# State space: the products u in a ring of three places, the third of them in SBUF, and three rows of C instead of four

## The reference, cut to what matters

```
a = jnp.exp(dt[..., None] * A[None, None])
u = dt[..., None] * Bv[:, :, None, :] * xs[..., None]
_, h = jax.lax.associative_scan(_affine_combine, (a, u), axis=1)   # h[t] = a[t] * h[t-1] + u[t]
y = jnp.einsum('btis,bts->bti', h, C) + xs * D_skip[None, None, :]
y = y * _silu(z)
return jnp.einsum('bti,di->btd', y, out_proj_w)
```

## Time and profile before

| | |
|---|---|
| median of 3 runs | 3406.47 us (3404.86 to 3411.97) |
| the profiled execution, its own time | 3401.26 us |
| its span, first to last instruction | 3399.5 us |
| state space: first scan to last scan | 2297.8 to 3381.3 us |
| a middle block of it | about 136 us |
| the last block | about 133 us |
| PE, DVE, ACT, POOL busy over the span | 94%, 82%, 68%, 47% |

### The profile page before, as it was taken

One profiled execution on the slowest core, in us unless ns is written; L12 is line 12 of the kernel. 1 busy time (PEld: TensorE's weight loads), 2 busy tenths in 40 slices (PEclk: granted clock), 3 DMA queues, 4 the chain that ended last, 5 costly groups with the idle time before them and its releaser, 6 DMA issues. The chain is left out here.

```text
span 3399.5 us, 61118 instructions
## 1 busy us (share of the span) xinstructions
PE 3188.7 (94%) x19814; PEld 1279.1 (38%) x19815; DVE 2788.6 (82%) x4945; ACT 2316.7 (68%) x3660; POOL 1601.0 (47%) x2080
## 2 busy tenths in 40 slices
PE   7997999989999999999999999769999999999987
PEld 4654666632222222222222222343334334333333
DVE  6766334689999999999999999258899989898997
ACT  4444333358887887888788788657877767777763
POOL 2113300024444434444333444207888888888885
PEclk9999999989999999999999999889999999999998
DMA  5442211111111110111111010141222222222221
GB/s 169 131 151 91 78 56 53 48 42 29 53 45 40 39 34 27 31 36 36 36 33 34 25 34 27 46 136 59 69 75 81 71 73 69 73 87 66 76 78 50
DMA packets 160889, 211.63 MB, mean 62 GB/s; under 512 B 32324, under 2 KB 108364, under 8 KB 160604
## 3 DMA queue, kind: packets, MB, share of 16 engines
q1 hardware_dynamic: 141340, 172.51, 16.6%
q0 software_dynamic: 8512, 18.76, 1.8%
q10 hardware_dynamic: 10752, 16.78, 1.5%
HBM read 154.48 MB, written 52.69 MB: 61 GB/s over the span
## 5 line engine op out<-in xcount | busy, mean ns | idle before, releaser
L1439 ACT ACTIVATE prob<-psS 128x1024 f32<-128x1024 f32 (+3 forms) x1280 | 1104.0, 906 | 280.2 <-PE psS L1623 270.8
L1489 DVE TENSOR_REDUCE pmax<-psR 128x1 f32<-128x512 f32 x1674 | 1057.2, 684 | 79.9 <-PE psR L1565 47.6
L2265 POOL TENSOR_TENSOR hc<-h_d,crep 128x512 f32<-128x512 f32 x512 | 647.7, 1273 | 186.8 <-DVE h_d L2494 136.5
L1565 PE MATMUL psR<-kslab,qslab 48*128 48x512 bf16 (+3 forms) x2480 | 653.0, 352 | 22.2 <-DVE pmax L1489 14.0
L1638 PE MATMUL psVo<-prob,vaug 128*32 128x512 f32 (+3 forms) x5120 | 630.8, 546 | 1.5 <-ACT ov L1443 0.8
L1623 PE MATMUL psS<-qslab,kslab 51*128 51x512 bf16 (+3 forms) x2560 | 533.4, 353 | 39.8 <-ACT prob L1439 22.6
L2494 DVE TENSOR_TENSOR_SCAN h_d<-a,state,psU 128x512 f32<-128x512 f32 x384 | 489.4, 1275 | 0.0
L1354 POOL TENSOR_SCALAR_AFFINE_SELECT prob<-prob 128x256 f32<-128x256 f32 (+1 forms) x512 | 214.0, 421 | 533.1 <-ACT prob L1439 533.1
L2484 DVE TENSOR_TENSOR psU<-dtx,psX 128x512 f32<-128x512 f32 x512 | 356.0, 695 | 89.6 <-PE psX L2644 38.8
L1565 PEld LDWEIGHTS psR<-kslab,qslab 48*128 48x128 bf16 x2480 | 187.3, 94 | 628.9 <-DVE pmax L1489 473.6
L2397 ACT ACTIVATE a<-dt,a_neg 128x512 f32<-128x512 f32 x512 | 366.7, 723 | 54.5 <-DVE h_d L2494 53.6
(11 more groups left out here) (351 smaller groups left out, 5045.5 us busy)
## 6 DMA issues: line engine op xcount, KB each, us to landing
crep<-c_rows_d SPq DMA_DIRECT2D x256, 256.0 KB, 3.1
x_e<-rows_d SPq DMA_DIRECT2D x72, 128.0 KB, 2.0
y_d<-y SPq DMA_DIRECT2D x72, 128.0 KB, 1.7
q_d<-parts SPq DMA_DIRECT2D x48, 128.0 KB, 2.4
k_d<-parts SPq DMA_DIRECT2D x48, 128.0 KB, 2.3
qslab<-q_d SPq DMA_DIRECT2D x60, 96.0 KB
kslab<-k_d SPq DMA_DIRECT2D x60, 96.0 KB
wg<-n_L_ffn_gate_proj_w_dram ACTq DMA_DIRECT2D x8, 512.0 KB, 4.1
```

Source lines behind the costliest of these rows:

```text
L1439: act.activation(prob[g % BUFS][:, :, off:BLK], psS[g % 2][:, :, off:BLK], ACT.Exp).then_inc(prob_ready, 1)
L1489: dve.tensor_reduce(into[:, lo:lo + (count - 1) * NEXT + 1:NEXT], psR[at % BANKS][:, 0:count * w].rearrange("p (n w) -> p n w", w=w), AX.X ...
L1565: ins = pe.matmul(dst[:, m * w:(m + 1) * w], qslab[u][rows, i * P:(i + 1) * P], kslab[u][rows, ch * BLK:ch * BLK + w], start=(m == 0), sto ...
L2265: pool.tensor_tensor(hc[:, g % CR], h[:, g % HR], crep[:, g // PAIR % SPR], ALU.mult).then_inc(hc_ready, 1)
```

## The change

The product u gets a third place: `u = [psU[0], psU[1], u_sb]`, where `u_sb` is a tile of 128 x 512 float32 in SBUF. Unit g uses place g % 3. `input_term(g)` now waits for `scan(g - 3)` instead of `scan(g - 2)`. Of the 512 units, 170 have their u in SBUF. The SBUF for it comes from the ring of C rows, which shrinks from four places to three; row k of C now waits until POOL has used up row k - 3.

```
-        AR, HR, CR, LAG, SPR = 5, 5, 6, 3, 4
+        AR, HR, CR, LAG, SPR = 5, 5, 6, 3, 3
...
         h = sb("h_d", [P, HR, BLK])
+        u_sb = sb("u_sb", [P, BLK])
...
         psU = [ps(f"psU{i}", [P, BLK]) for i in range(2)]
+        u = [psU[0], psU[1], u_sb]
...
                 dve.wait_ge(dtx_ready, CT * blk + c + 1 + CREDIT)
-                if g >= 2:
-                    dve.wait_ge(h_ready, g - 1 + CREDIT)
-                dve.tensor_tensor(psU[g % 2][:], dtx[:, c], psX[g // PAIR % 2][:], ALU.mult).then_inc(u_ready, 1)
+                if g >= len(u):
+                    dve.wait_ge(h_ready, g - len(u) + 1 + CREDIT)
+                dve.tensor_tensor(u[g % len(u)][:], dtx[:, c], psX[g // PAIR % 2][:], ALU.mult).then_inc(u_ready, 1)
...
-                dve.tensor_tensor_scan(h[:, g % HR], a[:, g % AR], psU[g % 2][:],
+                dve.tensor_tensor_scan(h[:, g % HR], a[:, g % AR], u[g % len(u)][:],
```

## The result

The changed kernel takes 3419.1 us (median of 18 runs, 3412.1 to 3427.5), the one before 3405.5 us (18 runs). The ratio is 1.0045, with a 95% interval of 1.0035 to 1.0056: 14 us slower, a quarter of the 52 us that were forecast. The profiled execution lies at the long end of its runs, 3426.2 us with a span of 3424.4, so what its rows add up to (25 us more than before) is more than the median shows.

The account below looks back on a forecast made before the run. DVE was taken to be close to the limit in every block. Per block, 12.8 us gained against 18.5 us of holds, plus waits, gave 143 instead of 136.3 us: 52 us more in all, forecast 3457 us, range 3325 to 3510.

Parts of the forecast that it names:

- The sum: State space phase: a block takes 143 us, 6.7 more than 136.3, adding 52 us over eight blocks.
- The first term: DVE's time in a block: 118.8 us after the removed wait plus 18.5 us of held scans, 137.3 us.
- the second: DVE's waits for others in a block: 2 to 5 us of the present 6 us stay.
- What bounds the kernel: State space phase: DVE close to the limit in all blocks, busy for 123.6 of 136 us in a middle one.
- the rival without a hold: Scans from SBUF are not held beside POOL; PE comes next, a block takes 126 us, 3326 us in all; 17 in 100.
- The gain of the removed wait: On DVE, the product behind a scan starts 0.20 us earlier a unit: 12.8 us a block, 102 us for 512 units.
- The hold: A scan with both streams in SBUF stands until POOL's instruction ends: 0.87 us each, 148 us for 170 scans.
- The threshold: Mean hold of a scan on DVE below 0.60 us, with POOL's sum under 136: the change wins; at 0.87 it loses.
- POOL's side: POOL's 112.2 us a block must share the way into SBUF with 27.1 us of scans, together 139.3 us.
- Three rows of C at nothing: Ring of C rows cut from four to three: rows still land with 2.5 us to spare, so no cost.

Follow-up runs that it names:

- the kernel with the old wait: The changed kernel, but each product waits for the scan straight ahead of it, as before the change: 3481.0 us, ratio 1.0226 to the kernel before.
- order of pairs: The kernel before (two PSUM places, four C rows) with DVE's order product, product, scan, scan for two units: 3390.0 us, ratio 0.9955.
- fills on POOL: The changed kernel with POOL's products with C replaced by two fills each: 3388.3 us; the kernel before with the same replacement and two C rows: 3401.6 us.
- the additions: Changed kernel with fills for POOL's products with C, plus every third unit a DVE maximum (3410.3 us), a POOL fill (3395.8 us) or both (3402.2 us).

## Why the prediction was right in its direction and wrong in its size

- The sum, where it failed. DVE's time in a block was to rise from 131.6 to 118.8 + 18.5 = 137.3 us, with 2 to 5 us of waits left beside it. The runs showed neither. DVE's own time stayed equal (1032.5 and 1030.9 us for the eight blocks), since the holds took 92.5 us and not 148. And the waits did not shrink to 2 to 5 us a block but grew from 8.3 to 11.6 (66.3 to 92.7 us in all). The first term was too large by 55 us, the second was taken with the wrong sign. The slower time that was forecast came, but through the waits for PE and not through the step that was to bring it; that the direction was right is in this part luck.
- What bounds the kernel. "DVE must be close to the limit" held in part: in the kernel with the old wait 77 of the 111 us by which DVE's own time grew came through. The step that failed is in the rival without a hold: PE "needs some 122 to 127" us a block. I took the times that PE's weight loads waited for room on PE. Those waits lie in the shadow of matmuls. In the same window the matmuls themselves waited for hardly anything (the first of three rows, 3.8 us in all):

```profile
PE psW L2591 <- ACT r L2389: 2.4, 1, 2.4
```

  The order of pairs shows a block near 135 us with PE full: 90 us less on DVE brought 15. The 3326 us of that rival would have been about 3390, as that kernel measured.
- The gain of the removed wait was 0.20 us a unit by the rows behind a scan. DVE's balance gives 94 us after and 90 us in the order of pairs, 0.18. The kernel with the old wait and the changed kernel are 62 us apart. The rule of the Trainium skill (VectorE: DVE Perf Modes, The DRAIN you can't avoid) that the wait costs nothing, by which they would be equal, doesn't hold for this pair of instructions.
- The hold. That a scan stands until POOL's instruction is over, and that POOL's is stretched in turn, is what the trace shows, and fills on POOL don't do it. With that the rule in the Trainium skill (SBUF, State Buffer, Who interferes with whom) is confirmed in both halves. The mis-sized term is "0.87 us lost" for each of 170 scans. It measured 0.54, 92.5 us instead of 148. Even where POOL's product does start right behind the scan ahead, as I had put it every time, a hold costs 0.65 to 0.7 us (1.93 instead of 1.27 us in the rows above): the scan ends 1.08 us after POOL's instruction and not a full 1.27. And POOL often runs out of step: 53 of the 170 scans lost less than 0.4 us, and POOL took part of the stops itself (100 us of stretching).
- The threshold. By my own ("Below 102/170 = 0.60 us on DVE, and with POOL's sum under 136, the change wins") a hold of 0.54 us, with POOL busy for 123 us a block, should have brought a small win. It lost 14 us. The threshold left out that DVE's waits for PE would grow, by 26 us in the profiled execution.
- POOL's side: its busy time in a block was to rise to 139 us; it rose to 123. 21 scans of 1.27 us take no more from it than the part in which it had something to do.
- Three rows of C at nothing: right.
- Why DVE waits more for PE at equal work is settled in part. The holds are the cause of the whole swing from 13 us faster to 14 slower; DVE's time makes 14 to 22 us of it by the additions. That POOL loses as much time to fills costs nothing before, and unevenness alone has no fixed sign. The rest, 9 to 17 us, appears only with true holds. The traces show what comes with them: POOL hands `hc` on 3.33 us after the scan's end instead of 2.08, and PE's matmuls wait 30.8 us for it instead of 8.7. That this chain makes the rest is argued, not shown: no addition made `hc` as late as the holds do. TensorE's lower clock stands beside it as a second candidate for a few us of the 14, and no run holds it fixed.

## What to carry to other kernels

A buffer that moves from PSUM to SBUF changes more than its capacity: where the instruction reads a second stream from SBUF, it and a GpSimd instruction that reads SBUF too stop for each other (0.54 us for each of 170 scans here). Before taking SBUF for a third place, look for another order that leaves two; here two products and then two scans remove the same gap with no memory at all and give 3390 us, the best full kernel of this study (3388 with seven places for hc, the same within its interval). And before counting a gain on the engine that waits least, relieve the next engine in one run: 90 us on DVE were worth 15 while PE was full and 55 when PE had some 12 us less to do in a block. Last, compare the granted clock of two profiles before their rows are subtracted from each other: here it differed by 29 us at the lower level.

## What the runs showed of the hardware

- A scan of 128 x 512 float32 with both streams in SBUF took 1275 ns beside POOL fills and 1.79 us on average beside POOL products; a POOL product beside it up to 2.27 us instead of 1.27. They take turns: 158 of 170 such scans end 1.08 or 1.09 us after a POOL instruction's end, and the 120 stretched POOL instructions end 0.94 to 1.08 us after a scan's end.
- The record of a held instruction starts when it would have started, and the hold is in its duration, not in idle time ahead of it. A view of idle times shows nothing of it.
- A DVE product that waits for nothing fresh is not only 0.2 us earlier behind a scan, it is recorded shorter too: 656 ns into SBUF and 668 into PSUM (medians) instead of 696, and the scan from PSUM behind it 1265 to 1269 instead of 1275.
- The same kernel's executions differ in the clock granted to TensorE and in time together: 3398.5 us on average at 0.979, 3411 at 0.974 (16 and 6 of 115 runs of the kernel before).
